# In the second attention layer, VectorE does a step's entries ahead of adding a tile to the row sums

## The reference

```python
# layer 0: full attention over 4096 pixels, softmax over i
q = Wq @ xf + bq; k = Wk @ xf + bk; v = Wv @ xf + bv      # 32, 32 and 256 rows
attn = softmax(einsum('bci,bcj->bij', q, k), axis=1)
x1 = gamma0 * einsum('bcn,bnm->bcm', v, attn) + xf
# layer 1: keys and values are 2x2 max-pooled to 1024 positions
theta = conv1x1(x1, theta_w, theta_b)                       # 32 rows, 4096 pixels
phi = maxpool2(conv1x1(x1, phi_w, phi_b))                   # 32 rows, 1024
g = maxpool2(conv1x1(x1, g_w, g_b))                         # 128 rows, 1024
attention = softmax(einsum('nid,ndj->nij', theta, phi), axis=-1)
y = gamma1 * conv1x1(einsum('ncj,nij->nci', g, attention), out_w, out_b) + x1
```

## The kernel before, in words

| step | entries (what VectorE does of them) |
|---|---|
| 0 | D2 of the chunk before: TensorE spreads the reciprocals (L1144), VectorE scales the output (L968; L959 twice in chunk 0) |
| 1, 3, 5 | ST: TensorE makes scores of chunk n+2 (L1131), VectorE takes their row maxima (L911). Chunks 0 to 5 only |
| 2, 3 | Z: output projection of the chunk before (L1148) |
| 5 | ZA: VectorE adds the second half of the output (L977), chunks 1 to 7, ahead of the step's ST |
| 7 | D1: TensorE sums `zc` over partitions (L1140), VectorE takes reciprocals (L938). Then ST, L911, and L917, L921, L922, L925, which send the maxima on to DMAs (L610) |

## Time and profile before

### The profile page before, as it was taken

The page is one execution under the profiler, slowest core; times in us unless marked ns, Lnnn a source line. Parts: engine busy times, 40 slices in busy tenths (PEclk is TensorE's granted clock), DMA queues, the critical chain, the costliest instruction groups (busy, mean ns, idle before and its releaser), DMA issues.

```text
span 2640.9 us, 38445 instructions
## 1 busy us (share of the span) xinstructions
PE 2578.1 (98%) x11696; PEld 2076.9 (79%) x11696; DVE 2034.4 (77%) x3384; ACT 1744.9 (66%) x3182; POOL 1942.5 (74%) x1528
## 2 busy tenths in 40 slices
PE   7999999999999999999999999999999999999988
PEld 6788888787778888877777888887777788888866
DVE  6788888777878878877787878787678687788766
ACT  6666666675776666666577666666658766666656
POOL 5777777665897777766688777777569877777767
PEclk9999999999999999999999999999999999999989
DMA  2000000110120000011022000001002100000012
GB/s 92 1 17 17 17 17 17 33 57 25 57 81 25 17 17 25 17 40 49 17 73 81 9 25 25 17 17 41 32 17 89 65 17 17 17 17 17 17 47 75
DMA packets 47658, 88.99 MB, mean 34 GB/s; under 512 B 5344, under 2 KB 5472, under 8 KB 47456
## 3 DMA queue, kind: packets, MB, share of 16 engines
q1 hardware_dynamic: 46896, 85.73, 9.7%
q10 hardware_dynamic: 560, 0.79, 0.1%
HBM read 52.70 MB, written 33.55 MB: 33 GB/s over the span
## 4 chain that ended last, share of the span: by engine, by line
PE 90%; DVE 4%; issue 2%; POOL 2%; ACT 1%; DMA 1%; SPq 0%; POOLq 0%; ACTq 0%; DVEq 0%
PE o_ps L1097 19%; PE o_ps L1094 19%; PE o_ps L1098 19%; PE aux L1131 11%; PE s_ps L1062 10%; PE aux L1108 3%; PE aux L1148 2%; PE aux L1165 2%; PE aux L1112 2%; PE aux L1144 1%; DVE mx L911 1%; POOL prob_l L658 1%; PE aux L1140 1%; DVE acc L873 1%; PE aux L1168 1%
## 5 line engine op out<-in xcount | busy, mean ns | idle before, releaser
L658 POOL TENSOR_TENSOR prob_l<-prob,prob_h 128x512 fp32r<-128x512 f32 x1280 | 1645.5, 1295 | 634.7 <-PE o_ps L1098 541.5
L717 ACT ACTIVATE prob<-s_ps 128x512 f32<-128x512 f32 x1280 | 767.8, 600 | 734.0 <-PE s_ps L1062 728.4
L911 DVE TENSOR_REDUCE mx<-aux 128x1 f32<-128x512 f32 x1256 | 860.0, 686 | 342.0 <-PE aux L1131 336.7
L1094 PE MATMUL o_ps<-prob_h,vh 128*128 128x512 f32 x2304 | 907.7, 394 | 3.6 <-issue 1.3
L1097 PE MATMUL o_ps<-prob_l,vh 128*128 128x512 f32 x2304 | 902.8, 392 | 2.7 <-POOL prob_l L658 2.0
L1098 PE MATMUL o_ps<-prob_h,vl 128*128 128x512 f32 x2304 | 899.6, 390 | 0.0
L873 DVE TENSOR_TENSOR acc<-prob,acc 128x512 f32<-128x512 f32 x1187 | 814.3, 686 | 55.1 <-ACT prob L717 35.9
L720 ACT ACTIVATE prob_h<-s_ps 128x512 fp32r<-128x512 f32 x1280 | 765.2, 598 | 0.0
L1062 PE MATMUL s_ps<-queries,keys 128*128 128x512 f32 x1280 | 521.9, 409 | 10.3 <-DMA queries<-nm_turned 7.7
L1131 PE MATMUL aux<-keys,queries 128*128 128x512 f32 x1256 | 509.0, 405 | 17.2 <-DVE mx L911 8.8
L1097 PEld LDWEIGHTS o_ps<-prob_l,vh 128*128 128x128 f32 x2304 | 433.0, 188 | 104.6 <-POOL prob_l L658 13.8
(11 more groups left out here) (125 smaller groups left out, 1647.8 us busy)
## 6 DMA issues: line engine op xcount, KB each, us to landing
xa<-x SPq DMA_DIRECT2D x32, 512.0 KB, 3.7
xp<-x SPq DMA_DIRECT2D x32, 512.0 KB, 3.6
spill<-xa SPq DMA_DIRECT2D x32, 512.0 KB, 2.8
xa<-spill SPq DMA_DIRECT2D x32, 512.0 KB, 3.6
y<-xa SPq DMA_DIRECT2D x32, 512.0 KB, 2.8
queries<-nm_turned SPq DMA_DIRECT2D x256, 1.0 KB
xp<-spill SPq DMA_DIRECT2D x3, 512.0 KB, 4.5
prob<-w_in ACTq DMA_DIRECT2D x1, 640.0 KB, 5.6
```

What stands on the lines that cost most here:

```text
L658: nc.gpsimd.tensor_tensor(out=prob_l[:, i, :], in0=prob[:, i, :], in1=prob_h[:, h % RING, :].bitcast(f32), op=ALU.subtract).then_inc(pl_re ...
L717: nc.scalar.activation(prob[:, h % PRING, :], s_ps[s][:, :], ACT.Exp).then_inc(p_ready, 1)
L911: ins = nc.vector.tensor_reduce(out=dst, in_=bank[:, :], axis=AX.X, op=ALU.max)
L1094: mm(out[:, :], value(vh, l, t, ct), prob_h[:, i, :], start=t == 0, stop=False)
```

## The change

One condition on VectorE decides, step by step, whether the addition of the tile two ahead comes before or after the step's entries. It now puts the entries first in every step of layer 1. Nothing is added, removed or changed on any other engine.

```diff
-                entries_first = t == KT[l] - SUM_AHEAD or l == 0 and n == NCH - 1 and b + 1 < B
+                entries_first = t == KT[l] - SUM_AHEAD or l == 1 or n == NCH - 1 and b + 1 < B
                 if not entries_first:
                     for h in begun_at(g, SUM_AHEAD):
                         add_prob(h)
```

## The result

The changed kernel takes 2679.36 us (median of 4 runs, 2677.19 to 2683.09); before, in the same comparison, 2643.49 us. The ratio is 1.0138, 95% interval 1.0122 to 1.0154. The direction was right, the size was not: 2664.3 was forecast, with 2674 as the upper end; the time lies 15 us above the forecast and 5 above that end. The profiled execution took 2677.19 us, 34.5 more than that of before, with a mean clock of 0.991 instead of 0.995.

The account below looks back on a forecast made before the run. TensorE, issued without a hole, was taken to set the period, so holes add to the time. 17 x 1.15 = 19.6, plus 1.4, 0.1 and 0.8, gave +21.9 us: 2664.3 us, range 2656 to 2674.

Parts of the forecast that it names:

- The last addition and its slots: VectorE, layer 1: tile n.7's addition takes the old copy's slot, ending at 740.64; L742 runs 1.86 us later.
- The hole: TensorE ahead of D1 in layer 1: D1 waits for L742, 1.15 us a chunk (1.05 to 1.27), in 17 chunks.
- the sum: All terms over layer 1's chunks in four images: 19.6 + 1.4 + 0.1 + 0.8, together +21.9 us.
- the other estimate, 0.95 us a chunk: VectorE's addition pair: by the skill's page L977 starts 0.2 us sooner, 3.4 us less in all.
- ScalarE and GpSimd without a price: Layer 1: exponentials of (n+1).1 reach GpSimd 1.65 us late, at no price, since TensorE is late itself.
- Rival 1: GpSimd does not catch up in layer 1: period grows 1.43 us, 2669, or the whole 1.86, 2676; chance 0.14.
- The places without a full hole: Chunk 1 of images 0 to 2: 0.48 us each; image 3's chunk 0: 0.1; chunks 6 and 7: no hole.
- The 0.2 us once an image: Chunks 6 and 7, where GpSimd sets the pace: addition of (n+1).1 releases its buffer 0.18 us late; 0.8 in all.
- the smaller terms: Layer 1 outside the 17 full holes: 1.4 for chunk 1, 0.1 for chunk 0, 0.8 once an image; 2.3 us.
- Rival 4: TensorE's clock falls behind the holes, adding 2.8 us a chunk in 17 chunks, 2712 us; chance 0.03.
- No change: TensorE in layer 1: a later wait absorbs the hole, time stays 2642; chance 0.06.
- rival 3: Layer 1: maxima ahead of additions free their banks sooner, saving 3.4 to 6.8 us, 2636 to 2639; chance 0.03.

Follow-up runs that it names:

- step5_only: Entries put ahead of the addition in step 5 of layer 1 alone, against the kernel before; 2656.78 us, ratio 1.0042.
- between: Full change, but in step 5 the addition stands between L977 and the maximum; 2660.67 us, ratio 1.0056 to the kernel before.
- all_but_step5: Entries put first in every layer 1 step except step 5, against the kernel before; 2650.27 us, ratio 1.0023.
- alternate: Kernel before with entries first in step 5 of chunks 3 and 5 as coded (text also says 3 and 4); 2651.26 us, ratio 1.0020.
- fill4: Full change plus four overwritten filling matmuls in front of D1 in layer 1's chunks 1 to 5; 2667.73 us, ratio 1.0087 to the kernel before.
- before_fill5: Kernel before plus five overwritten filling matmuls in front of D1 in layer 1's chunks 1 to 5; 2671.09 us, ratio 1.0090.
- fill2: Full change plus two overwritten filling matmuls in front of D1 in layer 1's chunks 1 to 5; 2668.54 us, ratio 1.0087 to the kernel before.
- d1_behind_st: Full change, but TensorE does step 7's ST ahead of D1 in chunks 0 to 5; 2664.23 us, ratio 1.0071 to the kernel before.

## Why the prediction was right, and where it was wrong

**The last addition and its slots: right.** Tile n.7 was to end 1.86 us later, L742 to start 0.09 behind it, with the slots before it unchanged. After, they are the same slots to 0.02 us.

**The hole: right in mechanism, a little small.** 1.15 us a chunk were forecast within 1.05 to 1.27, 1.2 are measured (12.95 against 11.75). It recurs in each chunk, and the loop from D1 to D1 is what repeats it. D1's load waits 24 times for 26.4 us, 1.1 each, where some 20 times and 20 us were forecast. step5_only, between, all_but_step5 and alternate each came out at the hole that the same counting of slots gives. In fill4, which has the delays but no falls, the blocks are 23.6 us longer; the sum had 21.9. The pair of additions takes 1.49 us again and L977 starts 1.40 behind its start, so the other estimate, 0.95 us a chunk, is out.

**ScalarE and GpSimd without a price: right.** before_fill5, which leaves their order alone, costs the same as fill4. Rival 1, at 0.14, is refuted: TensorE's loads waited for GpSimd's `prob_l` for 13.8 us before and for 9.3 after. (Its larger figure, 2676, lay outside the range that was to reach into it.)

**The places without a full hole: right.** Chunks 6 and 7 hold no hole; chunk 1 is looser. The 0.2 us once an image came too: chunk 7's L742 is 0.17 to 0.24 us later in fill4. Together with chunk 0 the smaller terms came to 4.6 us in fill4 (23.6 less 17 x 1.12) rather than 2.3, but the blocks hold the lower clock at image 3's turn as well, 1.5 us in before_fill5, which leaves 3.1.

**The clock: wrong, and this is the step that failed.** The sum has no term for falls of the clock, and they measured 9.4 us in six falls. Rival 4 got 0.03 with the words "A hole of 1.15 us lies nearer the second", that is, to a single wait of 0.57 us with no fall. The bounds there were 0.57 us (no fall) and 3.50 us (a fall), and nothing between. Taking the nearer end made an unknown into a certainty. The trace of before had more to offer than the one stretch that the prediction names: the clock was at 0.50 in two further places behind waits, from 49.9 us on and from 2517.7 us on, and at 1.00 behind the wait of 1.78 us shown above and others of 1.74 and 2.17. These would have spoken for no fall still more, and the other executions show that one trace can't tell: the same wait brings a fall in ten of fourteen.

The rival was also put as all or nothing, 17 chunks at 2.8 us, 2712, so that what came, a third of the holes at 1.57 us, stood in no case. The runs show: none in some 80 holes of 0.6 to 1.0 us (step5_only, between, fill2, alternate, d1_behind_st), 6, 8 and 2 in about 20, 20 and 8 holes of 1.2 us (one of the 6 and one of the 8 behind the shorter hole of chunk 1), 4 in some 20 of 1.8.

With 6 x 1.57 = 9.4 us, fill4's 23.6 and 17 x 0.1 for the hole that its period of 12.86 lacks against 12.96, 34.7 of the 35.3 us are told. Of the remaining 0.6, 0.4 lies at image 3's turn. Against the sum, the 35.3 are its 21.9, the 9.4 of the falls, 1.6 of that turn, 17 x 0.06 = 1.0 of the hole that was taken too small, and 1.4 in chunks 0 and 1 and smaller places.

The Trainium skill, TensorE: Matmul & The Clock Gate, section A second HAM failure mode: psum-queue depth-cycling, says that frequent short idle times between groups of matmuls can make the clock oscillate and cost throughput. The full change agrees, with six and eight falls; the kernels with holes of 1.0 us and less, as frequent, do not show it in their blocks.

**No change, and faster.** Neither came. That a reordering on an engine 77% busy, without more work, changes nothing was refuted: VectorE's busy time went from 2034.4 to 2036.0 us while the profiled execution grew by 34.5. The earlier maxima that rival 3 counts on don't exist; their slots are the same ones.

**What stays open.** Why one hole brings a fall and the next doesn't; why d1_behind_st has none; whether longer holes bring more of them.

## What to carry to other kernels

On an engine that is far from busy, ask which instruction another engine waits for, and count the slots ahead of that one only. A sum that is handed on at a fixed step has a deadline, and work that waits for the engine behind the deadline must not stand ahead of it. Where TensorE is issued without a hole, a new hole costs its length in every round, and in this kernel, where falls were seen behind matmuls 0.9 to 1.9 us apart, also a risk of the clock, which has to be priced as a share of the holes and not as all or none. One trace without a fall does not show that a wait is safe. If a hole can't be avoided, put work into it: here one matmul moved into it took away 4 us of holes, and its trace has no fall left.

## What the runs showed of the hardware that was not expected

- The clock fell to 0.50, its lower level of 1.2 GHz, behind waits of TensorE with its matmuls 1.3 us apart once in 12.9 us, though TensorE was busy for 12.01 of the 12.95 us of such a period. It cost 1.6 us each time. Twice it fell behind 1.0 us, in chunk 1.
- Eighty more matmuls made a kernel 12 us faster (fill4 against the full change), as its trace holds no fall where those of the full change hold six and eight.
- Which holes bring a fall differs between executions of one program; the four runs of the full change took 2677 to 2683 us at a clock of 0.991 down to 0.987, the longer the lower the clock. A wait of 1.78 us in layer 0, the same in all kernels, brought a fall in ten of fourteen executions.
